# A gated expert layer on one core: TensorE's register loads and two small matmuls change places in the last shared group

## The chip, the cores and the metric

The kernel runs on one core of one Trainium2 chip. The metric is the device time of one execution in microseconds (us); lower is better. The core's engines are TensorE (PE in the profile, its weight loads PEld), VectorE (DVE), ScalarE (ACT), GpSimd (POOL) and SyncE (SP). Each has a sequencer of its own that goes through the engine's instruction list in order; where the profile sets a q behind a name (PEldq), the work is the sequencer's.

## The reference

Two residual stages on `x` of shape [64 batches, 64 steps, 256]. The first adds a recurrent cell that is scanned over the 64 steps. The second adds a mixture of four experts of which each batch takes two, plus a shared expert that every batch takes:

```python
gate_scores = softmax(gate_logits * (1.0 + scale) + shift)      # [64, 4]
topk_w, topk_i = top_k(gate_scores, 2)                          # w_be: normalised weights, 0 where not chosen
for e in range(4):
    h = gelu(x @ ew1[e] + eb1[e]);  y = h @ ew2[e] + eb2[e]
    out = out + w_be[:, e][:, None, None] * mask[e][None, :, None] * y
shared = gelu(x @ sw1 + sb1) @ sw2 + sb2
x = x + out + shared
```

The gate's logits come from means of `x` over the steps, so that nothing of the gate can be known before the last step of the scan.

## The kernel before, in words

The features lie on the 128 partitions, as two halves, with the steps and the batches along the free dimension. Float32 products are made as three reduced ones: each operand is kept as a high and a low part, and high x high, high x low and low x high are added. An expert has a hidden width of 1024, cut into eight chunks of 128. `layer1` makes one chunk of hidden values of 512 tokens in six matmuls into a bank `hp`; ScalarE applies gelu (L386) and copies the high part (L393, semaphore `ghi_done`); VectorE or, in the last shared group, GpSimd (L338) subtracts to get the low part (`glo_done`); `layer2` then adds the chunk's share to the output in six matmuls into `zy`. All matmuls are recorded on line 825, that of a helper.

The 64 steps go in eight groups of eight. While the scan works on one group, TensorE does the shared expert on the group before. After the last step only group 7 of the shared expert is left. In the loop `for j in range(NCH)` on TensorE, chunk j's `layer1` is followed by `layer2` of chunk j - 2 (for j = 0 and 1 by what is left of the group before). In this loop the gate is worked out beside it:

- behind j = 0 TensorE makes the gate's logits; VectorE and ScalarE make scores and, at L618, the choice `sel` (semaphore `sel_done`); VectorE then works out the weights to L624.
- behind `layer2` of j = 2 TensorE waits for `sel_done` and makes two small products of `sel`, the position counts: the number of batches of each expert, and the place of each batch among them. Their semaphore `pos_mm` lets VectorE go on with `gate_slots` (L629 to L651): from the counts come the group bounds `starts` (L637, `starts_done`), and then the table `pick` (`pick_done`), whose last operations are the three of L651.
- behind `layer2` of j = 4 TensorE waits for `pick_done` and makes the list of batches with one small product (`lists`). VectorE adds an earlier shared output (L528), reads the list, and copies the tokens of the first routed group (L674, `gather_done`).

Routed groups follow. Their number for each expert is only known on the chip, so the loops over them have their bounds in registers. `group_bounds` loads the five entries of `starts` into registers of the engine that calls it, one by one: a TENSOR_LOAD, a register operation and a check of the range each (L209 in the profile). TensorE does so behind the shared loop, ScalarE, GpSimd and VectorE each behind their own share of it. The first two `layer1` of the first routed group lie between the last two `layer2` of the shared one (`turnover`).

Of the kernel before, what the change touches and what calls it, by code (L numbers as in the profile page):

```python
# [14 lines left out]
B = 64  # L15
# [3 lines left out]
E = 4  # L19
# [12 lines left out]
MAXG = (2 * B + (SLOTS - 1) * E) // SLOTS + 1  # L32
# [18 lines left out]


POS_AT, LIST_AT = 2, 4


C_TRI = 0
# [10 lines left out]
def cond_resid_kernel(nc, x, w0, w_exp, small, consts, out):  # L67
    ctx = ExitStack()
    with ctx:
        def sb(name, shape, dt=F32):  # L70
            return ctx.enter_context(nc.sbuf_tensor(name, shape, dt))
# [4 lines left out]
        def sem(name):  # L76
            return ctx.enter_context(nc.semaphore(name))
# [35 lines left out]
        con = sb("con", [P, C_END])  # L113
# [5 lines left out]
        ones_f = d_t[:].rearrange("p k b -> p (k b)")  # L119
# [4 lines left out]
        starts = sb("starts", [P, E + 1], I32)  # L124
# [6 lines left out]
        gp, lists = zy[:, 0], zy[:, 1]  # L131
# [12 lines left out]
        sel = gs[0:B, 42:46]  # L144
# [31 lines left out]
        sel_done, pos_mm, starts_done, pick_done, list_mm, batches_done = (  # L176
            sem(n) for n in ("sel_done", "pos_mm", "starts_done", "pick_done", "list_mm", "batches_done"))
# [8 lines left out]
        def w_of(i):  # L186

            return w_buf[i % 2]
# [14 lines left out]
                return stage[:, j % 2, 0:n]  # L203
            return g_f[:, j % 2, 0:n]

        def group_bounds(eng):

            eng.wait_ge(starts_done, 1)
            return [eng.value_load(starts[0:1, e:e + 1], min_val=0, max_val=MAXG) for e in range(E + 1)]  # L209

        def y_bank(r):

# [42 lines left out]
        def _(pool):  # L255
# [84 lines left out]
            def gather(r, q):  # L340
# [12 lines left out]
                last.then_inc(gather_done, 1)  # L353

            sv = group_bounds(pool)
            pool.wait_ge(batches_done, 1)
            for q in range(E):
# [8 lines left out]
        def _(act):  # L366
# [75 lines left out]
            for j in range(NCH):  # L442
                if j == 1:
                    act.wait_ge(nmax_done, 1)
                    act.activation(ex, logit, ACT.Exp, bias=nmax).then_inc(exp_done, 1)
                gelu_chunk(NG - 1, j, E, 512)
            sv = group_bounds(act)
            for q in range(E):
                e = ORDER[q + 1]
# [22 lines left out]
        def _(dve):  # L472
# [216 lines left out]
            gather_first()  # L689
            gate_weights()  # L690
            sv = group_bounds(dve)

            def weigh_phase(r, q, i):
# [129 lines left out]
        def _(pe):  # L823
            def mm(out_, lhsT, rhs, start, stop=False):
                return pe.matmul(out_, lhsT=lhsT, rhs=rhs, start=start, stop=stop, skip_group_check=True)  # L825
# [45 lines left out]
            def layer1(g, j, w, src, n, very_first=False):  # L871

                c = g * NCH + j
                if not very_first:
                    pe.wait_ge(gelu_done, c - 1)
                for k in range(K):
                    o = k * HID + j * P
                    hi, lo = src(0, k), src(1, k)
                    mm(hp[j % 2][:, 0:n], w[:, 0, o:o + P], hi, k == 0)
                    mm(hp[j % 2][:, 0:n], w[:, 1, o:o + P], hi, False)  # L880
                    last = mm(hp[j % 2][:, 0:n], w[:, 0, o:o + P], lo, False, k == K - 1)
                last.then_inc(l1_done, 1)

            def layer2(g, j, w, y, n):

                c = g * NCH + j
                pe.wait_ge(ghi_done, c + 1)
                for m in range(K):
                    o = WCOLS + j * D + m * P
                    mm(y[m][:, 0:n], w[:, 0, o:o + P], g_hi[:, j % 2, 0:n], j == 0)  # L890
                    mm(y[m][:, 0:n], w[:, 1, o:o + P], g_hi[:, j % 2, 0:n], False)
                pe.wait_ge(glo_done, c + 1)
                for m in range(K):
                    o = WCOLS + j * D + m * P
                    last = mm(y[m][:, 0:n], w[:, 0, o:o + P], g_lo[:, j % 2, 0:n], False, j == NCH - 1)
                    if j == NCH - 1 and m == 0:
                        last.then_inc(part_done, 2)
                last.then_inc(l2_done, 1)
# [16 lines left out]
            def group_src(g):  # L915
                return lambda part, k: x_hl[:, part, k, bass.ds(g * GT, GT), :]
# [55 lines left out]

            f = NG - 1
            pe.wait_ge(x1_done, T)
            for j in range(NCH):
                layer1(f, j, w_of(0), group_src(f), 512)
                if j >= 2:
                    layer2(f, j - 2, w_of(0), y_last, 512)
                else:
                    layer2(f - 1, NCH - 2 + j, w_of(0), y0, 512)  # L980
                if j == 0:
                    pe.wait_ge(agg_done, 1)
                    for i in range(3):
                        for k in range(K):
                            a = i * K + k
                            last = mm(gp[0:B, 0:E], agg[:, i, k], par[:, S_GW + E * a:S_GW + E * (a + 1)],
                                      a == 0, a == 3 * K - 1)
                    last.then_inc(gate_mm, 1)
                if j == POS_AT:
                    pe.wait_ge(sel_done, 1)  # L990

                    mm(gp[:, 2 * E:3 * E], ones_f[0:B], sel, True, True)
                    mm(gp[0:B, E:2 * E], con[0:B, C_TRI:C_TRI + B], sel, False, True).then_inc(pos_mm, 1)
                if j == LIST_AT:
                    pe.wait_ge(pick_done, 1)
                    mm(lists[0:32, 0:NSLOT], con[0:B, C_BIDX:C_BIDX + 32], pick, True, True).then_inc(list_mm, 1)


            sv = group_bounds(pe)

            def src_of(r, n):
                return lambda part, k: xg[:, bass.ds(r % 2, 1), part, k, 0:n].rearrange("p i n -> p (i n)")
# [115 lines left out]
```

## Time and profile before

| | us |
|---|---|
| median of 3 runs (lowest, highest) | 665.14 (664.55, 665.2) |
| the profiled execution, own time | 663.72 |
| its span, first to last instruction | 661.7 |
| TensorE busy | 641.8 (97%) |
| VectorE busy | 410.4 (62%) |
| ScalarE busy | 311.5 (47%) |
| GpSimd busy | 254.1 (38%) |

The span is what the trace covers; the profiled execution's own time is 2.0 us more than it. Busy times are of the whole span; the change touches a stretch of some 20 us in its middle, from about 322 to 342 us. The mean granted clock of TensorE over the span is 0.997 of the full 2.4 GHz.

### The profile page before, as it was taken

The page shows a single profiled execution, that of the slowest core. Times are in us where ns is not written, and L with a number is a line of the kernel's source. Part 1 is how long each engine was busy: PE and PEld are TensorE (multiplying, and loading weights), DVE is VectorE, ACT ScalarE, POOL GpSimd, SP SyncE. Part 2 cuts the span into 40 slices and gives each one's busy share as a digit, 9 for nine tenths or more (in the row PEclk, how much of TensorE's full clock was granted, in tenths as well). Part 3 has the DMA queues.
Part 4 walks back from the last instruction along what each step waited for, and adds up shares of the span by engine and source line. Part 5 has one row for each costly group of instructions (what it writes and reads, how often), then busy time and mean ns, then how long its engine had stood idle before and what let it go on. Part 6 is the DMA issues. An engine that isn't in the chain of part 4 may idle for free.

```text
span 661.7 us, 16380 instructions
## 1 busy us (share of the span) xinstructions
PE 641.8 (97%) x5732; PEld 551.6 (83%) x5732; DVE 410.4 (62%) x941; ACT 311.5 (47%) x521; POOL 254.1 (38%) x510
## 2 busy tenths in 40 slices
PE   7789999999999999999999999999999999999995
PEld 4678888888888888888778888888888899999995
DVE  5788865665656666577776644554456785555554
ACT  5444443434443344344546544444446664554460
POOL 1477654454454545333434333123311443311300
PEclk9999999999999999999999999999999999999998
DMA  7521100000000000000002100000001320000006
GB/s 264 200 67 49 51 16 2 0 0 0 0 0 0 0 0 0 0 2 2 0 1 81 48 0 0 0 0 0 0 0 58 93 60 0 0 0 0 0 1 255
DMA packets 7748, 20.71 MB, mean 31 GB/s; under 512 B 800, under 2 KB 1056, under 8 KB 7200
## 3 DMA queue, kind: packets, MB, share of 16 engines
q1 hardware_dynamic: 7424, 19.59, 8.8%
q10 hardware_dynamic: 288, 0.64, 0.3%
q8 instruction: 22, 0.36, 0.2%
q14 instruction: 14, 0.11, 0.1%
HBM read 16.03 MB, written 4.19 MB: 31 GB/s over the span
## 4 chain that ended last, share of the span: by engine, by line
PE 92%; DVE 3%; ACT 1%; DMA 1%; issue 1%; POOL 1%; DVEq 0%; SPq 0%; ACTq 0%
PE zy L825 55%; PE hp L825 37%; DMA acc<-in_x 1%; DVE d_t L511 1%; ACT uc L374 1%; DVE d_t L509 0%; DVE h_b L514 0%; DVE acc L770 0%; DVE y_all L651 0%; DVE y_all L698 0%; POOL x_hl L276 0%; ACT zy L369 0%; DVE w_buf L492 0%; DVE gs L633 0%; DVEq L770 0%
## 5 line engine op out<-in xcount | busy, mean ns | idle before, releaser
L485 DVE TENSOR_TENSOR g_lo<-g_f,g_hi 128x512 fp32r<-128x512 f32 (+1 forms) x168 | 125.2, 745 | 162.7 <-ACT g_hi L393 160.5
L825 PE MATMUL zy<-g_hi,w_buf 128*128 128x512 f32 (+1 forms) x704 | 184.6, 384 | 0.0
L393 ACT ACTIVATE g_hi<-g_f 128x512 fp32r<-128x512 f32 (+1 forms) x176 | 108.4, 616 | 152.2 <-PE zy L825 152.1
L386 ACT ACTIVATE g_f<-hp,first 128x512 f32<-128x512 f32 (+2 forms) x180 | 120.9, 672 | 120.8 <-PE hp L825 115.9
L825 PE MATMUL hp<-shared_buf,w_buf 128*128 (+1 forms) x720 | 173.6, 376 | 0.5 <-issue 0.5
L825 PEld LDWEIGHTS hp<-shared_buf,w_buf 128*128 128x128 f32 x720 | 135.0, 188 | 19.9 <-issue 1.1
L825 PEld LDWEIGHTS zy<-g_hi,w_buf 128*128 128x128 f32 x704 | 129.3, 188 | 19.7
L825 PEld LDWEIGHTS zy<-h_b,y_all 128*128 128x128 bf16 x3072 | 93.7, 98 | 25.3 <-issue 14.8
L825 PE MATMUL zy<-h_b,y_all 128*128 128x64 bf16 x3072 | 102.3, 193 | 8.2 <-DVE h_b L514 7.7
L825 PE MATMUL zy<-g_lo,w_buf 128*128 128x512 f32 (+1 forms) x352 | 106.0, 382 | 0.0
L825 PE MATMUL hp<-x_hl,w_buf 128*128 (+1 forms) x384 | 103.3, 404 | 1.0 <-POOL x_hl L276 1.0
L352 POOL CAST shared_buf<-x_hl x126 | 81.4, 694 | 0.0
L825 PEld LDWEIGHTS hp<-x_hl,w_buf 128*128 128x128 f32 x384 | 67.7, 189 | 13.2 <-POOL x_hl L276 1.5
L348 POOL TENSOR_TENSOR turn<-turn 128x1 f32<-128x1 f32 x14 | 3.1, 222 | 190.1 <-PE hp L825 185.5
L825 PEld LDWEIGHTS zy<-g_lo,w_buf 128*128 128x128 f32 x352 | 66.1, 188 | 11.8
L273 POOL TENSOR_TENSOR x_hl<-acc,first 128x128 f32 (+1 forms) x57 | 25.7, 451 | 113.8 <-DVE first L518 113.8
L825 PE MATMUL zy<-x_hl,shared_buf 128*128 (+1 forms) x384 | 56.4, 285 | 1.1 <-POOL x_hl L301 1.1
L825 PEld LDWEIGHTS zy<-x_hl,shared_buf 128*128 128x128 f32 x384 | 52.8, 189 | 5.2 <-DVE zy L547 1.5
L746 DVE TENSOR_TENSOR acc<-acc,y_all 128x128 f32 (+1 forms) x124 | 46.6, 415 | 14.0 <-issue 10.9
L374 ACT ACTIVATE uc<-zy 128x256 f32<-128x256 f32 x64 | 24.7, 385 | 51.2 <-PE zy L825 51.2
L492 DVE TENSOR_TENSOR w_buf<-stage,w_buf 128x512 fp32r<-128x512 f32 x40 | 32.6, 827 | 0.0
L295 POOL TENSOR_TENSOR seg<-seg,acc (+1 forms) x64 | 32.0, 500 | 0.6
(126 smaller groups left out, 438.0 us busy)
## 6 DMA issues: line engine op xcount, KB each, us to landing
stage<-in_w_exp SPq DMA_DIRECT2D x40, 256.0 KB, 2.9
out_y<-acc SPq DMA_DIRECT2D x2, 1376.0 KB, 4.7
acc<-in_x SPq DMA_DIRECT2D x1, 2048.0 KB, 8.2
acc<-in_x SPq DMA_DIRECT2D x1, 1536.0 KB, 9.8
out_y<-acc SPq DMA_DIRECT2D x1, 1344.0 KB, 5.8
acc<-in_w SPq DMA_DIRECT2D x1, 512.0 KB, 4.5
acc<-in_x SPq DMA_DIRECT2D x1, 512.0 KB, 6.7
acc<-in_w ACTq DMA_DIRECT2D x1, 512.0 KB, 5.5
```

What stands on the lines that cost most here:

```text
L273: pool.tensor_tensor(hi, a, h_f[:, 1 - i % 2], ALU.add).then_inc(x1_hi, 1)
L295: pool.tensor_tensor(sg, sg, a, ALU.add).then_inc(seg_done, 1)
L348: pool.tensor_tensor(turn[:, 1:2], turn[:, 0:1], turn[:, 0:1], ALU.mult)
L352: last = pool.tensor_copy(dst, tokens_of(x_hl, e, bs[s]))
L374: act.activation(uc[:], zb[:, buf, :, :, i % QT, :], ACT.Tanh).then_inc(tanh_done, 1)
L386: act.activation(raw_of(j, n, keep), hp[j % 2][:, 0:n], ACT.Gelu_apprx_tanh, bias=par[:, S_B1 + e * NCH + j:S_B1 + e * NCH + j + 1]).then_ ...
L393: act.activation(chunk_of(j, n, keep)[0], raw_of(j, n, keep), ACT.Copy).then_inc(ghi_done, 1)
L485: dve.tensor_tensor(lo, raw_of(j, n, keep), hi.bitcast(F32), ALU.subtract).then_inc(glo_done, 1)
L492: dve.tensor_tensor(w[:, 1, c:c + PIECE], stage[:, n % RING], w[:, 0, c:c + PIECE].bitcast(F32), ALU.subtract).then_inc(piece_done, 1)
L511: dve.scalar_tensor_tensor(out=d_t[:], in0=uc[:, 0], scalar=1.0, in1=d_t[:], op0=ALU.add, op1=ALU.mult).then_inc(q_done, 1)
L746: dve.tensor_tensor(dst, dst, y_w[:, :, s * n:(s + 1) * n].rearrange("p k (a n) -> p k a n", a=RUNS[e][1]), ALU.add).then_inc(add_done, 1 ...
L825: return pe.matmul(out_, lhsT=lhsT, rhs=rhs, start=start, stop=stop, skip_group_check=True)
```

## The change

Two things change, both in TensorE's instruction list within the loop over the last shared group. The loads of the five group bounds are taken from behind the loop and put behind `layer1` of chunks 5, 6 and 7: two, two and one. The wait for `sel_done` and the two small products of the position counts go from behind `layer2` to between `layer1` and `layer2` of the same turn, j = 2. The other engines' lists stay as they are.

```diff
+BOUNDS_AT = {5: (0, 1), 6: (2, 3), 7: (4,)}
...
-        def group_bounds(eng):
+        def group_bounds(eng, which=range(E + 1)):
 
             eng.wait_ge(starts_done, 1)
-            return [eng.value_load(starts[0:1, e:e + 1], min_val=0, max_val=MAXG) for e in range(E + 1)]
+            return [eng.value_load(starts[0:1, e:e + 1], min_val=0, max_val=MAXG) for e in which]
...
             pe.wait_ge(x1_done, T)
+            sv = []
             for j in range(NCH):
                 layer1(f, j, w_of(0), group_src(f), 512)
+                if j in BOUNDS_AT:
+                    sv += group_bounds(pe, BOUNDS_AT[j])
+                if j == POS_AT:
+                    pe.wait_ge(sel_done, 1)
+
+                    mm(gp[:, 2 * E:3 * E], ones_f[0:B], sel, True, True)
+                    mm(gp[0:B, E:2 * E], con[0:B, C_TRI:C_TRI + B], sel, False, True).then_inc(pos_mm, 1)
                 if j >= 2:
                     layer2(f, j - 2, w_of(0), y_last, 512)
...
-                if j == POS_AT:
-                    pe.wait_ge(sel_done, 1)
-
-                    mm(gp[:, 2 * E:3 * E], ones_f[0:B], sel, True, True)
-                    mm(gp[0:B, E:2 * E], con[0:B, C_TRI:C_TRI + B], sel, False, True).then_inc(pos_mm, 1)
                 if j == LIST_AT:
                     pe.wait_ge(pick_done, 1)
                     mm(lists[0:32, 0:NSLOT], con[0:B, C_BIDX:C_BIDX + 32], pick, True, True).then_inc(list_mm, 1)
 
-
-            sv = group_bounds(pe)
```

## Rows read from the trace of the kernel before

**Rows 1.** The page: busy times; the scan's small matmuls (busy us, mean ns).
```profile
PE 641.8 (97%) x5732; PEld 551.6 (83%) x5732; DVE 410.4 (62%) x941; ACT 311.5 (47%) x521; POOL 254.1 (38%) x510
...
L825 PE MATMUL zy<-h_b,y_all 128*128 128x64 bf16 x3072 | 102.3, 193 | 8.2 <-DVE h_b L514 7.7
```

**Rows 2.** TensorE's waits, 318 to 347 us: total us, times, longest.
```profile
PE hp L825 <- issue: 0.5, 1, 0.5
PE zy L825 <- DVE y_all L651: 0.3, 1, 0.3
```

**Rows 3.** Waits of 347 to 661.7 us: the longest one of TensorE.
```profile
PEld zy L825 <- issue: 0.4, 1, 0.4
```

**Rows 4.** Timeline, TensorE: start us, us, instructions [idle before, releaser].
```profile
322.52 1.52 PE L825 MATMUL hp<-x_hl,w_buf 128*128 128x512 f32 x6
...
325.33 0.38 PE L825 MATMUL zy<-gs,d_t 64*128 64x4 f32 x2
...
325.85 1.65 PE L825 MATMUL hp<-x_hl,w_buf 128*128 128x512 f32 x6
...
328.70 1.52 PE L825 MATMUL hp<-x_hl,w_buf 128*128 128x512 f32 x6
...
331.93 0.52 PE L825 MATMUL zy<-y_all,con 64*32 64x200 f32 x2 [0.34 <-DVE y_all L651]
...
332.38 1.67 PE L825 MATMUL hp<-x_hl,w_buf 128*128 128x512 f32 x6
...
333.67 0.88 PEld L825 LDWEIGHTS zy<-g_hi,w_buf 128*128 128x128 f32 x4
...
335.27 1.52 PE L825 MATMUL hp<-x_hl,w_buf 128*128 128x512 f32 x6
...
337.99 1.52 PE L825 MATMUL hp<-x_hl,w_buf 128*128 128x512 f32 x6
...
341.36 1.62 PE L825 MATMUL hp<-shared_buf,w_buf 128*128 128x512 f32 x6 [0.49 <-issue]
```

**Rows 5.** Line 209 on TensorE's sequencer: ns min/median/max, first and last start us.
```profile
L209 PEldq TENSOR_LOAD <-starts x5: 299/310/487, 337.7 to 340.6; - x5
...
L209 PEldq SEQ_ASSERT  x5: 18/18/32, 338.5 to 341.2; - x5
```

**Rows 6.** Timeline, VectorE's part of the gate.
```profile
323.56 0.16 DVE L618 TENSOR_SCALAR gs<-gs 64x4 f32<-64x4 f32 x1
...
324.50 0.22 DVE L624 TENSOR_SCALAR gs<-gs 64x4 f32<-64x4 f32 x1
...
326.02 0.16 DVE L629 COPY gs<-zy 128x4 f32<-128x4 f32 x1 [1.30 <-PE zy L825]
...
326.67 0.93 DVE L633 TENSOR_SCALAR gs<-gs 128x4 f32<-128x4 f32 x1
...
328.52 0.16 DVE L644 TENSOR_SCALAR gs<-gs 64x4 f32<-64x4 f32 x1
...
329.63 2.24 DVE L651 SCALAR_TENSOR_TENSOR y_all<-con,gs,y_all 64x200 f32<-64x200 f32 x3
```

**Rows 7.** Timeline, GpSimd's low parts of chunks 1, 2 and 3.
```profile
324.75 1.28 POOL L338 TENSOR_TENSOR g_lo<-g_f,g_hi 128x512 fp32r<-128x512 f32 x1 [3.65 <-ACT g_hi L393]
...
326.27 1.30 POOL L338 TENSOR_TENSOR g_lo<-g_f,g_hi 128x512 fp32r<-128x512 f32 x1 [0.24 <-ACT g_hi L393]
...
329.73 1.47 POOL L338 TENSOR_TENSOR g_lo<-g_f,g_hi 128x512 fp32r<-128x512 f32 x1 [2.16 <-ACT g_hi L393]
```

**Rows 8.** Timeline, what feeds TensorE behind the shared group.
```profile
334.50 4.18 DVE L674 CAST shared_buf<-x_hl 128x256 fp32r x8 [1.05 <-issue]
...
344.37 0.69 ACT L386 ACTIVATE g_f<-hp,first 128x512 f32<-128x512 f32 x1 [2.77 <-issue]
...
346.43 0.69 DVE L485 TENSOR_TENSOR g_lo<-g_f,g_hi 128x512 fp32r<-128x512 f32 x1 [2.88 <-ACT g_hi L393]
...
349.73 0.42 PEld L825 LDWEIGHTS zy<-g_lo,w_buf 128*128 128x128 f32 x2
```

## The prediction

> **What bounds the kernel now.** I read the page first: TensorE is busy for 97% of the span, the next engine for 62% [rows 1]. The reader is to see that only time in which TensorE is idle can be won here, since the change takes no work off it. Then TensorE's waits around the place of the change: from 318 to 347 us there are two, 0.5 us put down to "issue" and 0.3 us to VectorE's L651 [rows 2]; behind that, no wait of TensorE is longer than 0.4 us up to the end [rows 3]. The timeline places the two: 0.34 us ahead of the list product at 331.93, and 0.49 us ahead of the first routed `layer1` at 341.36 [rows 4]. The second is the group bounds: five loads on TensorE's sequencer start from 337.7 to 340.6 and the last check is at 341.2 [rows 5].
>
> The idle figures understate the price, for matmuls overlap. An undisturbed turn of the loop, twelve matmuls, takes 337.99 - 335.27 = 2.72 us [rows 4]. Against it:
> - 337.99 to 341.36 is 3.37: the loads cost 0.65.
> - 332.38 to 335.27 is 2.89: a start after an interruption costs 0.17 more in the turn behind it.
> - 322.52 to 325.85 is 3.33: the position counts, for which TensorE does not wait, cost 0.61, of which 325.85 - 325.33 = 0.52 is from their first matmul on; so 0.09 goes into the change of tile.
> - 328.70 to 332.38 is 3.68: the list product costs 0.96. From its first matmul on it takes 332.38 - 331.93 = 0.45; with 0.09 for the change of tile that is 0.54 without a wait. 0.42 is the price of waiting for `pick`.
>
> **Part 1, the loads leave the end of the loop.** The sequencer runs far ahead of the array: the first load starts at 337.7, before `layer1` of chunk 7 starts at 337.99 [rows 4, 5], and that `layer1` and the `layer2` behind it stand ahead of the load in the list. Five loads take from 337.7 to 341.2; the array runs dry at about 340.9. With the loads gone from there, the sequencer can hand over the routed `layer1` three us before it is wanted. Gain: 0.65, and the slow start behind it, 0.17, together 0.82. That `layer1` reads what L674 gathers, and this ends at 334.50 + 4.18 = 338.68, before 341.36 - 1.2 = 340.2 [rows 4, 8]: it is not the next thing to be late.
>
> **Part 2, the loads come in at three places.** Nothing else is queued behind them on TensorE but the `layer2` of the same turn, and no other engine waits for them. They cost nothing where the array has work in its queue for as long as they take. One load with its checks is 338.5 - 337.7 = 0.8 us for the first, and (341.2 - 338.5) / 4 = 0.68 for each further one [rows 5], so two take 1.48.
> - Chunk 5 is the tight one, as the sequencer has just been held for `pick_done`. From its release it hands over list product and `layer1`, 8 pairs or fewer; the scan's small matmuls show that a pair can go in 102.3 / 3072 = 0.033 us [rows 1], so 0.26; then 1.48 for the loads: 1.74. The array wants the weights of `layer2` at 333.67, which is 1.74 behind the list product's start at 331.93 [rows 4]. So it is a tie; with some 0.05 us from the semaphore, the stall is 0.05. Where `pick` comes before the array is ready, the loads have that much more room and it is zero. Bounds: below zero isn't possible, as nothing is removed here; above, 0.3 (the pairs handed over at twice that price). I take 0.05.
> - Chunks 6 and 7: each turn gives 2.72 us and the loads take 1.48 and 0.8, so the sequencer gains over a us per turn. Cost 0. If that cover were gone (a queue that doesn't run ahead), chunks 5 to 7 would cost 1.48 + 1.48 + 0.8 = 3.76.
>
> The Trainium skill ("DMA: Bandwidth & Descriptors", Latency and other measured facts) gives a load into registers a floor of about 600 ns. The rows show 299 to 487 ns for it [rows 5]. With 600 ns and the same checks behind it (0.38), two loads would be 1.96 and chunk 5 would stall for 0.5; the trace has durations, so they are used, and the page differs.
>
> **Part 3, the position counts go ahead of `layer2`.** The two products cost the same 0.61 at either place. They must find `sel` ready: L618 ends at 323.56 + 0.16 = 323.72 [rows 6]. Undisturbed, the next matmul would start half a turn behind 322.52, at 323.88, and the counts 0.09 later, at 323.97. Slack 0.25, enough for the semaphore; stall 0. If `sel` were late by more than that, the stall would be the excess, and `layer2` would stand behind it. `layer2` of chunk 0 ends 0.6 later, so ScalarE's copy of chunk 2's high part and GpSimd's low part of it slip by as much (from 326.27 to about 326.8, [rows 7]); `layer2` of chunk 2 wants this behind 330: no cost.
>
> **What it brings.** The counts are ready at 323.97 + 0.6 = 324.6 in place of 325.95. VectorE is free at 324.50 + 0.22 = 324.72, so L629 starts 1.26 us earlier than 326.02 [rows 6]. How much of this reaches `pick` depends on GpSimd. In the trace VectorE's L633 takes 0.93 where its like take 0.16 (L644); it starts at 326.67, and GpSimd's subtraction covers 326.27 to 327.57 [rows 6, 7]. Likewise the three L651 take 2.24 across GpSimd's 329.73 to 331.20. So such an operation waits until GpSimd's has nearly ended. After the change GpSimd's chunk 1 covers 324.75 to 326.03: L629 gets in ahead of it or reads PSUM beside it, the comparison L630 (two operands in SBUF, as in L651) waits to about 325.9. Then L630 to L636, some 0.2 each, run to about 326.8, without the 0.78 that L633 waited before. GpSimd's chunk 2 now starts there and is met by L637 or by L644, which waits to about 328.0. L644 would then end at 328.1 in place of 328.68: 0.58 earlier. Of L651 the first two run ahead of or into GpSimd's 329.73 and the third waits behind it, as one did before: `pick` comes at about 331.3 to 331.45 in place of 331.88. Bounds: 0 (L637 waits as well, and the chain is where it was) and 1.26. The array could take the list product at 331.93 - 0.42 = 331.51. So a gain of `pick` of 0.42 is enough; more brings nothing. I take 0.42, range 0 to 0.42.
>
> The rule in the Trainium skill ("SBUF — State Buffer", SBUF: two separate sides) is that GpSimd and a VectorE operation with two SBUF inputs or in a two-port mode shut each other out for the whole instruction. L641, with one input from PSUM, would by it not wait; no row shows such an operation beside GpSimd. If L641 did wait, `pick` would gain the same, for L644 waits for the same end.
>
> **The sum.** 0.82 + 0.42 - 0.05 = 1.19, so 1.2 us off 663.72, the profiled execution: 662.5. The median of the runs is 1.42 above that execution; off 665.14 the same sum gives 663.95. Does it last to the end? TensorE has next to no waits behind 347 [rows 3]. What it needs earlier now: the first routed chunk's gelu at 344.37 + 0.69 = 345.06 stands behind ScalarE's own loads, and is wanted by `layer1` of chunk 2, two turns behind 340.2, at 345.6; its low part is made at 346.43 + 0.69 = 347.12, and wanted at 349.73 - 1.2 = 348.5 [rows 8]. Both hold, the first by 0.5. I take off 0.1 for small things that move (the changes of tile, GpSimd's order): 664.05.
>
> **The rivals.**
> - The list product gains nothing: GpSimd swallows the earlier start, and only the loads' 0.82 is won, less 0.1 to 0.3 at chunk 5, for the sequencer is then released no earlier than the array. For it: three of VectorE's operations in this chain can meet GpSimd. Against it: the 0.78 us of L633 goes in every order that I can lay out. 665.14 - 0.6 = 664.5. Chance 0.2.
> - Given back: the array arrives earlier at the routed groups, and waits there for engines that kept their time. For it: ScalarE and VectorE load the five bounds themselves, 2.77 and 2.88 us idle [rows 8]. Against it: the slacks of 0.5 and 1.4 above. 665.1. Chance 0.1.
> - Slower: the loads lie open in the midst of the array's work. The mechanism is that the queue is not full at chunk 5, being just released, and that a load holds back the weights behind it. Full price 3.76 - 0.82 - 0.42 = 2.5, so 667.6; it is slower than before from the point at which more than 1.24 us of the 3.76 lie open, say both loads of chunk 5 with little ahead of them. Against it: the sequencer was 3 us ahead at 337.7. Chance 0.07.
> - Faster than the sum: the whole chain shifts by its 1.26, and further waits of TensorE that the trace puts down to no one go as well; 663.4. Against it: I find nothing more to win than 1.24. Chance 0.1.
>
> My own forecast has the rest, 0.53, with a range of 663.7 to 664.4.
>
> **How the numbers follow.** A measurement of this kernel can tell about 0.2%, 1.33 us, from no change: faster is below 663.81, slower above 666.47. The forecast's gain of 1.1 is under this bound, but near it. Faster: the last rival's 0.1 and about 0.1 of the forecast's, 0.2. Slower: the 0.07 of the open loads. Same: 0.73. The range 663.4 to 665.3 takes in all but the slower rival and the tails of the others, 0.15 left out.
>
> **What would show it.** Right: `layer1` of the routed group follows within 2.8 us on that of chunk 7, with no idle time put down to issue; the list product starts 2.8 us behind `layer1` of chunk 4, with none for L651; L633 takes 0.2; the loads of chunk 5 end before the array wants `layer2` of chunk 3. Wrong: a wait for L618 ahead of the counts; idle time ahead of `layer2` of chunks 3, 4 or 5; a new wait of TensorE between 345 and 350; L651 ending at 331.9 as before.

## The result and the profile after

The changed kernel takes 662.88 us in the median of 6 runs (662.59 to 663.41), the kernel before 665.09 us in runs beside it (6 runs, 664.55 to 666.52). The ratio is 0.9966, 95% interval 0.9954 to 0.9978: 2.2 us faster. Forecast were 664.05 us, 1.1 us faster, and a range of 663.4 to 665.3. The gain is twice the forecast, and the time lies below the range.

The profiled execution of the changed kernel took 663.41 us, only 0.3 us less than that of before (663.72). So the two traces side by side show a seventh of what the medians show, and the first thing to settle is what they say about each other.

The trace of the changed kernel has a span of 661.4 us, and TensorE is busy for 642.8 of them (97%).

Waits of TensorE from 318 to 347 us, all there are (against [rows 2]):

```profile
PE zy L826 <- DVE y_all L652: 0.2, 1, 0.2
```

The timeline of TensorE in the changed kernel (one line number up, against [rows 4]): start, length, instructions:

```profile
323.18 1.52 PE L826 MATMUL hp<-x_hl,w_buf 128*128 128x512 f32 x6
...
324.63 0.38 PE L826 MATMUL zy<-gs,d_t 64*128 64x4 f32 x2
...
326.64 1.52 PE L826 MATMUL hp<-x_hl,w_buf 128*128 128x512 f32 x6
...
329.36 1.52 PE L826 MATMUL hp<-x_hl,w_buf 128*128 128x512 f32 x6
...
332.40 0.52 PE L826 MATMUL zy<-y_all,con 64*32 64x200 f32 x2 [0.17 <-DVE y_all L652]
...
332.86 1.66 PE L826 MATMUL hp<-x_hl,w_buf 128*128 128x512 f32 x6
...
335.72 1.52 PE L826 MATMUL hp<-x_hl,w_buf 128*128 128x512 f32 x6
...
338.44 1.52 PE L826 MATMUL hp<-x_hl,w_buf 128*128 128x512 f32 x6
...
341.16 1.52 PE L826 MATMUL hp<-shared_buf,w_buf 128*128 128x512 f32 x6
```

The reader is to see four things. From chunk 7 to the routed `layer1` it is 341.16 - 338.44 = 2.72 us, an undisturbed turn: the loads' gap is gone. The turn of chunk 5, which now holds two loads, takes 335.72 - 332.86 = 2.86, against 2.89 before: no stall. The turn of the list product takes 332.86 - 329.36 = 3.50 in place of 3.68: 0.18 won, and 0.17 us of waiting left. The counts' turn is 3.46, 0.13 more than before, and the one behind it 2.72, 0.13 less. From the `layer1` of chunk 2 to the routed one it is 17.98 us in place of 18.84; with the slow start of 0.12 that followed the gap, the stretch has gained 0.98 us.

The rest of the difference between the traces lies ahead of the change: `layer1` of chunk 2 starts at 323.18 and not at 322.52. This takes 0.66 off the 0.98, and 0.3 is what the two traces show. The windows of 12 to 60 us show where it comes from (length; busy us of TensorE, its weight loads, VectorE, ScalarE and GpSimd with their instructions; granted clock; DMA share and GB/s), the kernel before first:

```profile
12.00:60.00 48.00, 39.08 (x718) 34.09 (x717) 38.53 (x101) 22.95 (x52) 29.55 (x55) 1.00 0.36 117
```

and the changed kernel:

```profile
12.00:60.00 48.00, 39.71 (x694) 34.84 (x693) 38.19 (x101) 22.36 (x50) 28.78 (x53) 0.96 0.35 117
```

The clock granted in these 48 us was 0.96 in the execution of the changed kernel, and TensorE did 694 of its matmuls in them and not 718. That is an accident of an execution and not of the change: of the eleven profiles of this case three have 0.96 there, one of them of the unchanged kernel, and in these `layer1` of chunk 2 starts at 323.08 to 323.21; the other eight have 1.00 and start it at 322.34 to 322.62. So the profile of after is 0.5 us above its median. That of before is 1.4 us below its own, and this is the 1.42 us that the prediction noted and did not explain.

### The profile page after: what moved, and what is told of

Its sections match the earlier page's. It is cut to its first block, busy times and chain, and to the rows that moved or that the text cites. A ratio compares the mean times of both kernels' runs of the same rounds, so it can differ in the third digit from the quotient of the medians.

```text
span 661.4 us, 16380 instructions
## 1 busy us (share of the span) xinstructions
PE 642.8 (97%) x5732; PEld 553.1 (84%) x5732; DVE 411.9 (62%) x941; ACT 311.2 (47%) x521; POOL 254.9 (39%) x510
## 4 chain that ended last, share of the span: by engine, by line
PE 91%; DVE 4%; ACT 1%; DMA 1%; issue 1%; POOL 1%; DVEq 0%; SPq 0%; ACTq 0%
PE zy L826 55%; PE hp L826 36%; DMA acc<-in_x 1%; ACT uc L375 1%; DVE d_t L512 1%; DVE d_t L510 0%; DVE h_b L515 0%; DVE acc L771 0%; DVE y_all L652 0%; DVE y_all L699 0%; POOL x_hl L277 0%; DVE gs L600 0%; DVE h_r L631 0%; ACT zy L370 0%; DVE w_buf L493 0%
```

## The experiments

My theory after reading the result (A in the expectations) was that the medians are right and the 1.2 us that the stretch does not show belong to one of the two edits; the rival (B) was that they are scatter between executions. The kernel before was timed again beside each.

| kernel | median us | kernel before | ratio (95% interval) |
|---|---|---|---|
| loads moved alone | 662.85 | 664.94 | 0.9965 (0.9952 to 0.9979) |
| counts moved alone | 664.71 | 664.94 | 0.9994 (0.9985 to 1.0003) |
| the kernel before, again | 664.83 | 664.94 | 0.9998 (0.9989 to 1.0007) |
| the changed kernel, again | 662.79 | 664.94 | 0.9967 (0.9955 to 0.9979) |
| all five loads behind chunk 7 | 662.99 | 664.90 | 0.9976 (0.9967 to 0.9985) |
| all five loads behind chunk 5 | 664.65 | 664.90 | 0.9996 (0.9987 to 1.0005) |
| the kernel before, copies give way | 663.78 | 664.90 | 0.9984 (0.9975 to 0.9993) |
| changed, list half a turn later | 662.65 | 664.90 | 0.9969 (0.9956 to 0.9981) |
| changed, copies give way | 662.78 | 664.96 | 0.9965 (0.9952 to 0.9979) |

**The loads alone.** The changed kernel with the counts put back behind `layer2`:

```diff
                 layer1(f, j, w_of(0), group_src(f), 512)
                 if j in BOUNDS_AT:
                     sv += group_bounds(pe, BOUNDS_AT[j])
-                if j == POS_AT:
-                    pe.wait_ge(sel_done, 1)
-                    mm(gp[:, 2 * E:3 * E], ones_f[0:B], sel, True, True)
-                    mm(gp[0:B, E:2 * E], con[0:B, C_TRI:C_TRI + B], sel, False, True).then_inc(pos_mm, 1)
                 if j >= 2:
...
+                if j == POS_AT:
+                    pe.wait_ge(sel_done, 1)
+                    mm(gp[:, 2 * E:3 * E], ones_f[0:B], sel, True, True)
+                    mm(gp[0:B, E:2 * E], con[0:B, C_TRI:C_TRI + B], sel, False, True).then_inc(pos_mm, 1)
                 if j == LIST_AT:
```

> Only the loads of the group bounds move; the position counts stay behind layer 2. The trace of the changed kernel gives the loads' gap 0.65 us plus 0.12 us of slow start behind it. Theory A (the 2.2 us between the medians are this gap, the list product's shorter wait, and something outside the stretch that the change made): 0.8 us faster than before by the profile of 322 to 342 us, and if the unexplained 1.2 us belongs to the loads, 2.0. Theory B (the 1.2 us that the stretch does not show is scatter between executions of the kernel before): 0.8 us faster within 0.4.

It was 2.09 us faster than before. All but about 0.1 us of the gain is the loads'.

**The counts alone.** The kernel before, with the same four lines put between `layer1` and `layer2`:

```diff
                 layer1(f, j, w_of(0), group_src(f), 512)
+                if j == POS_AT:
+                    pe.wait_ge(sel_done, 1)
+                    mm(gp[:, 2 * E:3 * E], ones_f[0:B], sel, True, True)
+                    mm(gp[0:B, E:2 * E], con[0:B, C_TRI:C_TRI + B], sel, False, True).then_inc(pos_mm, 1)
                 if j >= 2:
```

> Only the position counts move ahead of layer 2; the loads stay behind the loop. The trace of the changed kernel shows the list product's wait shorter by 0.18 us and nothing else. Theory A: 0.2 us faster by the stretch, and 1.4 if the unexplained part belongs to the counts. Theory B: 0.2 us faster, within the measurement's noise.

0.23 us faster, with an interval that takes in no change. The trace has the list product's idle time at 0.17 us, as in the changed kernel, so that by the trace the counts do bring their 0.2 us; the medians can't tell it from nothing.

**The kernel before, again.**

> The kernel before against itself. Both theories: no difference; what it shows is the noise of a comparison. Theory B expects single executions that scatter by 1 us or more, and profiled ones to lie below those that are timed.

664.83 against 664.94: the comparison is good to a tenth of a us. Its profile is what the case turned on. ("The shown execution" is from here on the one profiled before the change, whose rows stand ahead of the prediction.) TensorE's idle time at the loads (the last bracket of its timeline below) is 1.7 us and not the 0.5 of [rows 2]; the counts-alone kernel, which has the loads at the old place too, has 1.6. Line 209 on TensorE's sequencer, in the kernel before, again, shows that the loads take as long as before, but start 1.8 us later (against [rows 5]), 1.1 us more than the 0.7 by which this whole execution is late:

```profile
L209 PEldq TENSOR_LOAD <-starts x5: 300/308/493, 339.5 to 342.5; - x5
```

And the timelines of TensorE, GpSimd and VectorE there:

```profile
338.65 1.52 PE L825 MATMUL hp<-x_hl,w_buf 128*128 128x512 f32 x6
...
343.21 1.62 PE L825 MATMUL hp<-shared_buf,w_buf 128*128 128x512 f32 x6 [1.68 <-issue]
...
336.97 2.52 POOL L338 TENSOR_TENSOR g_lo<-g_f,g_hi 128x512 fp32r<-128x512 f32 x1 [2.54 <-ACT g_hi L393]
...
335.19 3.13 DVE L674 CAST shared_buf<-x_hl 128x256 fp32r x8 [1.04 <-issue]
```

The same of the shown execution of the kernel before (the eight gather copies took 4.18 us there [rows 8]), the second row the one copy that lies in 336.8 to 337.2:

```profile
336.31 1.34 POOL L338 TENSOR_TENSOR g_lo<-g_f,g_hi 128x512 fp32r<-128x512 f32 x1 [2.57 <-ACT g_hi L393]
...
336.41 1.52 DVE L674 CAST shared_buf<-x_hl 128x256 fp32r x1
```

Here the reader sees the mechanism. GpSimd subtracts for the low part of chunk 5 while VectorE makes its eight gather copies back to back, one every 0.38 us. In the shown execution GpSimd got in between two copies: its operation took 1.34 us, the next copy took 1.52, and all eight 4.18. In the other it stood outside until the last copy: 2.52 us, and the eight copies 3.13. That low part ends at 339.49, and at 339.5 the first load starts; in the shown execution it ends at 337.65, and the first load starts at 337.7. In the counts-alone kernel the two times are 338.42 and 338.5. The sequencer was held at `layer2` of chunk 5 by its wait for `glo_done`, with the loads behind. From chunk 7's `layer1` to the routed one this makes 343.21 - 338.65 = 4.56 us in place of 3.37: the loads' gap costs 1.84 us against an undisturbed turn, not 0.65.

The times add up: 663.72 of the shown execution, 1.19 for the longer gap and 0.69 for the later start of chunk 2 make 665.60, and this profiled execution took 665.62. Without the 0.69 it is 664.91, the median. By its time the shown execution is a rare one: of the 76 timed executions of the kernel before on record one took 663.47 and all others 664.55 or more.

**The changed kernel, again.**

> The changed kernel again. Theory A: 2.2 us faster than before once more. Theory B: 1.0 us faster (0.65 + 0.12 + 0.18 from its trace), and the first result was 1.2 us of luck.

2.15 us faster once more. B's reading of the 2.2 us as luck falls; its other half holds, that one profiled execution is not the typical one. GpSimd's operation takes 2.5 us in this profile, in the first one of the changed kernel and in that of the loads alone: the collision is there in all of them, and TensorE has no gap. The row of the first one:

```profile
336.76 2.50 POOL L339 TENSOR_TENSOR g_lo<-g_f,g_hi 128x512 fp32r<-128x512 f32 x1 [2.36 <-ACT g_hi L394]
```

**Where the loads must stand.** Two more places for them, in the kernel with the loads alone moved:

```diff
-BOUNDS_AT = {5: (0, 1), 6: (2, 3), 7: (4,)}
+BOUNDS_AT = {7: (0, 1, 2, 3, 4)}
```

> Counts as before; all five loads stand behind layer 1 of chunk 7, thus ahead of layer 2 of chunk 5 and its wait for GpSimd's low part of chunk 5. Theory A (the sequencer reaches the loads only when that low part is done, which GpSimd has late because VectorE's gather copies shut it out; what counts is to stand ahead of that wait): as fast as with the loads spread out, 2.1 us faster than before; the loads run from about 335.5 to 339. Theory C (the gain comes from spreading the loads, since five in a row outlast the queue): five in a row cost 3.5 us against 2.7 us of work in the queue, so 0.8 us or more is lost again, 1.3 us faster at most.

1.91 us faster; line 210 on TensorE's sequencer:

```profile
L210 PEldq TENSOR_LOAD <-starts x5: 298/310/490, 335.4 to 338.3; - x5
```

Its trace has the turn of chunk 7 at 340.77 - 338.05 = 2.72, undisturbed. Five loads in a row cost the array nothing, if they start at 335.4, ahead of the wait for `glo_done`. Theory C, that they had to be spread, falls by this trace; the interval of the ratio, 1.0 to 2.2 us faster, would by itself leave room for the 1.3 us of C. With `{5: (0, 1, 2, 3, 4)}` instead:

> Counts as before; all five loads stand behind layer 1 of chunk 5, where the sequencer has just been released by the list's wait. 3.5 us of loads against 1.7 us of work handed over: the array should run dry for 1.7 us ahead of layer 2 of chunk 3, with 0.1 us of slow start. Theory A: 2.1 - 1.8 = 0.3 us faster than before. If a load doesn't hold back the matmuls behind it: 2.1 us faster.

0.25 us faster, with an interval that takes in no change. The timeline of TensorE:

```profile
332.94 1.66 PE L826 MATMUL hp<-x_hl,w_buf 128*128 128x512 f32 x6
...
335.99 1.19 PE L826 MATMUL zy<-g_hi,w_buf 128*128 128x512 f32 x4 [1.39 <-issue]
...
337.47 1.52 PE L826 MATMUL hp<-x_hl,w_buf 128*128 128x512 f32 x6
```

The turn takes 4.53 us in place of 2.85: 1.68 lost, where 1.7 was expected from 3.5 us of loads against what had been handed over since the list's wait. This is the slower rival's mechanism, and it is real; two loads at this place cost nothing, five cost this.

**The collision taken away.** The kernel before, with VectorE giving way in the midst of the copies:

```diff
                 for s in range(SLOTS):
+                    if s == SLOTS // 2:
+                        dve.wait_ge(glo_done, (NG - 1) * NCH + 6)
                     dst = xg[:, 0, :, :, s * n:(s + 1) * n].rearrange(
```

> The kernel before, with one wait more: VectorE, halfway through the eight gather copies, waits until GpSimd's low part of chunk 5 is done. Theory A: GpSimd's operation takes 1.3 us in place of 2.5, the loads start 1.1 us earlier, the gap ahead of the routed layer 1 falls from 1.7 to 0.5 us: 1.1 us faster than before, about 663.8. If the length of the gap has another cause than GpSimd's operation: no change, or slower by what the copies are later.

663.78 us, 1.12 faster than before, by a wait added on another engine. The timelines of GpSimd, VectorE and TensorE, and the loads:

```profile
336.28 1.29 POOL L338 TENSOR_TENSOR g_lo<-g_f,g_hi 128x512 fp32r<-128x512 f32 x1 [2.52 <-ACT g_hi L393]
...
334.51 1.62 DVE L676 CAST shared_buf<-x_hl 128x256 fp32r x4 [1.04 <-issue]
337.69 1.61 DVE L676 CAST shared_buf<-x_hl 128x256 fp32r x4 [1.57 <-POOL g_lo L338]
...
341.28 1.63 PE L827 MATMUL hp<-shared_buf,w_buf 128*128 128x512 f32 x6 [0.43 <-issue]
...
L209 PEldq TENSOR_LOAD <-starts x5: 295/309/492, 337.6 to 340.5; - x5
```

GpSimd's low part ends at 337.57, the first load starts at 337.6, and the gap is 0.43: the course of the shown execution of the kernel before, now made to happen. That execution took 663.72 us, and this kernel's median is 663.78. The same wait in the changed kernel:

> The changed kernel with the wait of the experiment on the gather copies (VectorE waits halfway until GpSimd's low part of chunk 5 is done). Theory A: GpSimd's operation falls from 2.5 to 1.3 us here too, but nothing waits for it any more, since TensorE wants that low part only 0.7 us after its late end: no change against the changed kernel, 2.1 us faster than before. If GpSimd's delay costs by a second way beside the loads: up to 1 us faster than the changed kernel.

662.78 against 662.79 and 662.88, GpSimd's operation takes 1.29 us, and from the `layer1` of chunk 2 to the routed one it is 340.50 - 322.52 = 17.98 us, as in the changed kernel. With the loads out of its way the delay costs nothing that can be seen, so in the kernel before it cost by way of the loads.

**The list product later.** The list product goes to the place that the counts got, between `layer1` and `layer2`, in turn 5, and the loads to chunks 6 and 7:

```diff
-BOUNDS_AT = {5: (0, 1), 6: (2, 3), 7: (4,)}
+BOUNDS_AT = {6: (0, 1, 2), 7: (3, 4)}
...
                 layer1(f, j, w_of(0), group_src(f), 512)
+                if j == LIST_AT + 1:
+                    pe.wait_ge(pick_done, 1)
+                    mm(lists[0:32, 0:NSLOT], con[0:B, C_BIDX:C_BIDX + 32], pick, True, True).then_inc(list_mm, 1)
                 if j in BOUNDS_AT:
...
-                if j == LIST_AT:
-                    pe.wait_ge(pick_done, 1)
-                    mm(lists[0:32, 0:NSLOT], con[0:B, C_BIDX:C_BIDX + 32], pick, True, True).then_inc(list_mm, 1)
```

> The changed kernel, with the list product half a turn later, between layer 1 of chunk 5 and layer 2 of chunk 3, and the loads behind layer 1 of chunk 6 (three) and 7 (two). The list product's wait, 0.17 us idle and some 0.24 us in all, goes; the gather copies start 1.4 us later and end at about 339.5, still ahead of 340.9 where the array wants them. 0.2 us faster than the changed kernel, 2.4 faster than before. If the later copies shut GpSimd out at another chunk as well: slower by the wait that this makes, up to 1 us.

662.65 us. TensorE's timeline has the list product without a wait:

```profile
332.86 0.52 PE L826 MATMUL zy<-y_all,con 64*32 64x200 f32 x2
```

The copies run from 334.82 to 337.95. Counted from the `layer1` of chunk 2 they start 0.5 us later than in the changed kernel, not 1.4 as expected, though the list product is 1.1 us later: in the changed kernel VectorE was busy with L529 to 333.67 and read the list only then, and here it is done with L529 at 333.0 and waits 0.42 us for the product. GpSimd's low part of chunk 5, which arrives earlier among the copies, takes even 3.3 us, and TensorE has no gap for it. The stretch from chunk 2 to the routed `layer1` is 340.26 - 322.51 = 17.75 us, 0.23 less than in the changed kernel, and the medians differ by 0.14 and 0.23. Differences of this size between medians are at the edge of what they tell: that the list product's wait is gone is shown, that the kernel is faster by it is not.

## Why the prediction was wrong

- **The loads leave the end of the loop: right mechanism, the term mis-sized.** "Gain: 0.65, and the slow start behind it, 0.17, together 0.82." Moved alone the loads gave 2.09 us; from the trace of the kernel before, again, 1.84 + 0.12 = 1.96 (the slow start behind the gap is 0.12 and not 0.17). With the 0.18 of the list product this makes 2.14, against 2.21 and 2.15 of the medians. The step that failed is the price of the old place, 0.65, and with it the sentence that the sequencer "runs far ahead of the array: the first load starts at 337.7". It ran ahead only as far as its next wait, that of `layer2` of chunk 5 for GpSimd's low part, and 337.7 was the end of that low part. I took 337.7 as a property of the queue, when it was the end time of another engine's operation, and that operation is in a contest with eight copies of VectorE. In the shown execution it won, and the gap was 0.5 us; in the two other profiles with the loads at the old place it lost, and the gap was 1.6 and 1.7.
- **The 1.42 us between the profiled execution and the median.** I noted it and carried the sum over unchanged. 1.2 of it was this very term. The question to ask of such a trace is which of its waits could have been longer.
- **The loads at their three new places: right.** 0.05 at chunk 5 was forecast, nothing was found (2.86 and 2.85 us against 2.89). The way of counting loads that lie open was right as well: 1.68 us for five behind chunk 5, where it gives 1.7. The 600 ns of the Trainium skill ("DMA: Bandwidth & Descriptors", Latency and other measured facts) does not fit any run here, 295 to 494 ns, nor the stall of 0.5 us that it would have made at chunk 5.
- **The counts: right that they are free, too much hoped from them.** They started at 324.63, where 323.97 plus the trace's later start of 0.66 puts them, without a price. L631 met GpSimd's chunk 1 (1.13 us) and L645 its chunk 2 (0.89), as forecast, and L630, which reads PSUM, took 0.16 us beside GpSimd's operation. Counted from the `layer1` of chunk 2, the three L652 began 0.36 us earlier than the three L651 before. But the second of them waits for GpSimd's chunk 3, in both kernels (1.33 us before, 1.51 after), and not the third as I had it; and GpSimd's operation ended only 0.18 us earlier, at 331.68. So `pick` came 0.18 us earlier, not 0.42 or more; the list product gained 0.18, and the medians give 0.23, not distinguishable from nothing.
- **The rivals.** Faster than the sum had 0.1, for the wrong reason: I had looked for waits that the trace does not name. The contest itself was in the text, for L633 and L651, and in the Trainium skill's rule ("SBUF — State Buffer", SBUF: two separate sides). I used it only in one direction, GpSimd holding up VectorE. Here VectorE held up GpSimd for 1.2 us, and the wait stood on TensorE's path. The rule's lock for a whole instruction agrees with the copy of 1.52 us; that GpSimd stayed outside for several copies in a row goes further than one instruction.

What stays open: what decides who gets in. GpSimd's operation started 0.10 us before the recorded start of the next copy where it won, and 0.12 to 0.16 before it in the seven profiles where it lost; one case on the one side doesn't make a rule.

## What to carry to other kernels

Instructions that only feed a sequencer belong ahead of its next wait for another engine, not behind it: here their cost was then hidden even though that engine was late. They need enough work queued in front of them all the same; right behind a wait just ended, five of them cost 1.68 us. Before a gap is priced from one trace, find what released its first instruction and ask how steady that is; here a median 1.4 us above the profiled execution was the sign that it was not. A kernel can be made faster by having one engine wait, where that lets another finish earlier that is waited for.

## What was not expected of the hardware

- GpSimd's subtraction of 1.3 us takes 2.5 us when it arrives amid back-to-back copies of VectorE, as it waits for the last of them and not for the one under way. In the shown execution of the kernel before it got in, and a copy, 0.46 us otherwise, took 1.52. In the kernel with all five loads behind chunk 5 it arrived behind the last copy and took 1.28, and the eight copies 3.06.
- Five register loads in a row on TensorE's sequencer, 3.4 us, cost the array nothing when the sequencer starts on them early enough (335.4 to 338.8), and 1.7 us when it has just been released (332.5 to 335.9).
- Two executions of the same program can differ by 0.7 us (323.21 against 322.52 for the `layer1` of chunk 2) before the change is reached: the granted clock from 12 to 60 us is 0.96 in the later one and 1.00 in the other, and all eleven profiles of this case divide in this way.
